# Operand rows of two attentions fetched from SBUF head by head instead of through DRAM

## The reference

```python
def _L0_attn_a_ref(x, Wq, Wk, Wv, Wo):        # windowed attention
    q, k, v = (proj(Wq), proj(Wk), proj(Wv))
    scores = jnp.einsum('bnsd,bntd->bnst', q, k) * scale
    mask = _longformer_mask(S)                # |i - j| <= 16, token 0 sees all and is seen by all
    scores = jnp.where(mask[None, None], scores, jnp.float32(-jnp.inf))
    attn = jax.nn.softmax(scores, axis=-1)
    out = jnp.einsum('bnst,bntd->bnsd', attn, v)
    return jnp.einsum('bsh,oh->bso', out.transpose(0, 2, 1, 3).reshape(B, S, H), Wo)
...
    x = x + windowed attention; + ternary FFN; + bidirectional gated recurrence; + ternary FFN
    x = x + full attention (_L1_attn_a_ref); x = x + mixture of experts
    x = x + full attention (_L1_attn_b_ref); x = x + mixture of experts
```

## Time and profile before

| | |
|---|---|
| median of 3 runs | 1111.35 us |
| profiled execution | 1111.73 us, its span 1110.0 us, mean granted TensorE clock 0.94 |
| TensorE (PE) busy | 1001.4 us, 90% |
| VectorE (DVE) busy | 833.8 us, 75% |
| ScalarE (ACT) busy | 747.5 us, 67% |
| GpSimd (POOL) busy | 154.9 us, 14% |
| DMA | 60386 packets, 64.47 MB, mean 58 GB/s; HBM read 27.06 MB, written 35.32 MB |

### The profile page before, as it was taken

How to read it: one execution, slowest core, us unless ns; L and a number is a source line. 1 busy time by engine, 2 the same in 40 slices (tenths; PEclk the granted TensorE clock), 3 DMA queues, 4 the chain that set the end, 5 groups by cost and what they waited for, 6 DMA issues and landing times.

```text
span 1110.0 us, 32515 instructions
## 1 busy us (share of the span) xinstructions
PE 1001.4 (90%) x13424; PEld 460.4 (41%) x13437; DVE 833.8 (75%) x1030; ACT 747.5 (67%) x1490; POOL 154.9 (14%) x430
## 2 busy tenths in 40 slices
PE   6699999688769999999899899999989999999897
PEld 2445455333342344444344344434434344443344
DVE  4546654447647999999778789977879997898732
ACT  3514446265440999998767789876779986697781
POOL 8200000036000000000102110010211001010000
PEclk8889999889869999999989899989999998999899
DMA  3753442100044323201000044200004420010000
GB/s 105 211 180 86 109 103 60 37 0 1 1 146 141 70 51 77 56 18 27 14 10 15 20 129 105 57 12 13 13 23 129 106 53 12 12 40 21 11 26 24
DMA packets 60386, 64.47 MB, mean 58 GB/s; under 512 B 17424, under 2 KB 39184, under 8 KB 60112
## 3 DMA queue, kind: packets, MB, share of 16 engines
q1 hardware_dynamic: 60240, 62.40, 21.3%
HBM read 27.06 MB, written 35.32 MB: 56 GB/s over the span
## 4 chain that ended last, share of the span: by engine, by line
DVE 51%; PE 37%; ACT 4%; DMA 3%; issue 3%; SPq 1%; ACTq 0%; DVEq 0%
DVE nmf L1670 42%; PE wide L685 24%; PE bank L685 13%; DVE xcsq L1441 1%; DMA KQs<-mw_dram 1%; ACT L1196 1%; DVE xp L1441 1%; ACT big L1196 1%; ACT scr L1196 1%; DVE xcsq L1450 1%; SPq L445 1%; DVE nmt L1609 1%; DMA x<-xT 1%; DVE res L1441 1%; DVE big L1822 0%
## 5 line engine op out<-in xcount | busy, mean ns | idle before, releaser
L1670 DVE TENSOR_REDUCE nmf<-wide 128x1 f32<-128x1024 f32 x512 | 591.2, 1209 | 54.7 <-PE wide L685 54.2
L1196 ACT ACTIVATE big<-wide 128x512 f32<-128x512 f32 x683 | 391.4, 601 | 100.7 <-PE wide L685 90.0
L685 PE MATMUL wide<-big,KQs 48*128 48x512 bf16 (+1 forms) x1376 | 359.7, 351 | 4.3 <-DVE nmf L1670 3.0
L685 PE MATMUL bank<-big,V 128*9 128x128 f32 x8192 | 329.5, 280 | 11.2
L685 PE MATMUL wide<-KQs,big 50*128 50x512 bf16 (+1 forms) x1035 | 274.2, 331 | 8.1 <-ACT big L1196 8.1
L685 PEld LDWEIGHTS bank<-big,V 128*9 128x9 f32 x8192 | 178.2, 91 | 239.0 <-ACT big L1196 188.8
L1196 ACT ACTIVATE big<-bank 128x512 f32<-128x512 f32 (+1 forms) x469 | 232.7, 515 | 46.8 <-PE bank L685 41.3
L685 PE MATMUL bank<-KQs,big 50*128 50x512 bf16 x341 | 133.8, 392 | 3.9 <-ACT big L1196 3.9
L685 PEld LDWEIGHTS wide<-KQs,big 50*128 50x128 bf16 x1035 | 70.1, 95 | 116.5 <-ACT big L1196 61.7
L1196 ACT ACTIVATE scr<-wide 128x380 f32<-128x380 f32 (+3 forms) x128 | 61.2, 486 | 81.2 <-PE wide L685 70.0
L618 POOL CAST nms<-nmf 128x4 bf16<-128x4 f32 x128 | 23.8, 186 | 651.8 <-DVE nmf L1670 651.8
(11 more groups left out here) (214 smaller groups left out, 802.7 us busy)
## 6 DMA issues: line engine op xcount, KB each, us to landing
o_dram<-big SPq DMA_DIRECT2D x128, 64.0 KB
big<-kf_dram SPq DMA_DIRECT2D x32, 200.0 KB
kf_dram<-scr SPq DMA_DIRECT2D x24, 256.0 KB, 3.4
qf_dram<-scr SPq DMA_DIRECT2D x24, 256.0 KB, 3.7
KQs<-qf_dram SPq DMA_DIRECT2D x32, 192.0 KB
ow_dram<-scr SPq DMA_DIRECT2D x32, 142.5 KB
big<-kw_dram SPq DMA_DIRECT2D x16, 275.0 KB
kw_dram<-scr SPq DMA_DIRECT2D x12, 352.0 KB, 5.6
```

The costliest lines, as they stand in the source:

```text
L685: return nc.tensor.matmul(o, l, r, start=start, stop=stop, **kw)
L1196: return nc.scalar.activation(o, i, f, **kw)
L1670: nc.vector.tensor_reduce(nmf[:, i % 4, c:c + 1], wide[:, k:k + 2, :].rearrange("p g c -> p (g c)"), AX.X, ALU.max, negate=True).then_inc( ...
```

## The change

The four DRAM tensors of operands and all stores into them go. A part tensor now has four blocks instead of three: the first part stands twice (`AGAIN`), in such an order (`BLOCK`) that the six products of q's and k's parts are two runs of three adjacent blocks on each side. One DMA (`rows_in`) reads three adjacent blocks of one head's 8 partitions and writes 24 operand rows; a head takes two DMAs for k and two for q. The rows of ones are written into the operands directly. Batch 1's parts get buffers of their own (in `big` and `xcsq`; `s0` and `xwin` move). SP's order is rewritten: windowed, the heads of batch 0 at once when its parts are there, those of batch 1 one a unit; full, twelve heads of batch 0 before the first shift, then one a slot, and batch 1's in slots 4 to 15; in layer 2 one head a slot from slot 19 of the run on.

Beside this: the repeated first part is copied by VectorE (windowed, in `third`) and by POOL (full, `fp_again`, `c_again`); token 0's scores are six bf16 products of parts instead of one fp32 product with `kf`; ScalarE waits for all 16 heads of batch 0 (`op_in`) before its first windowed weight; fillers go from 22 to 8 and from 24 to none; `true_x` runs before `project_full`, and TensorE's first full maxima no longer wait for batch 1's residues.

```diff
-ROW_PARTS = ((2, 1, 0, 1, 0, 0), (0, 1, 2, 0, 1, 0))
+BLOCK = ((1, 2, 3), (2, 1, 0))
+AGAIN = (0, 3)
+PRODUCTS = ((3, 2), (2, 2), (2, 1), (1, 2), (1, 1), (1, 0))
...
-        partk = partw[:, 0:3 * KW].rearrange("p (n c) -> p n c", n=3)
-        partq = partw[:, 3 * KW:3 * (KW + QW)].rearrange("p (n c) -> p n c", n=3)
+        partk = [blocks(scr, 0, KW), blocks(big, o, KW)]
+        partq = [blocks(scr, 2 * KW, QW), blocks(xcsq, 0, QW)]
...
-        partf = scr[:, 0:3072].bitcast(BF16).rearrange("p (n i c) -> p n i c", n=2, i=3)
+        partf = [[blocks(t, 2 * S * i, S) for i in range(2)] for t in (scr, xcsq)]
...
+        HEADS = [4 * g + odd + 2 * j for g in range(H // 4) for odd in range(2) for j in range(2)]
...
+            def ones_rows_in(t):
+                cols = t.shape[1] * t.shape[2] // 64
+                for r in (KR, KR + 1, 64 + KR, 64 + KR + 1):
+                    row = t[r:r + 1, :, :].rearrange("r n c -> r (n c)").rearrange("r (a c) -> r a c", c=cols)
+                    sp.dma_start(row, onesb[:, 0:cols]).then_inc(ones_in, 16)
+
+            def rows_in(dst, r, k, h, src, signal):
+                for a in range(2):
+                    o = a if k else 1 - a
+                    sp.dma_start(dst[r + KR // 2 * a:r + KR // 2 * (a + 1)], src[D * h:D * h + D, o:o + 3, :]).then_inc(signal, 16)
...
+                def load_head(b, h):
+                    p, r, s = h // 2, 64 * (h % 2), op_in[2 * (4 * b + h // 4) + h % 2]
+                    rows_in(kopw[:, p, KW * b:KW * b + KW], r, 0, h, partk[b], s)
+                    rows_in(qopw[:, p, QW * b:QW * b + QW], r, 1, h, partq[b], s)
...
+                sp.wait_ge(part3, 2 * len(WG))
+                for h in HEADS[0:H // 2]:
+                    load_head(0, h)
                 sp.wait_ge(win_const, 1)
                 for u in range(AHEAD_W - 1):
+                    for h in HEADS[H // 2 + 2 * u:H // 2 + 2 * u + 2]:
+                        load_head(0, h)
                     turned(u, mw_dram[u, :, :])
                     if u:
                         shift(u - 1)
...
-                    if u in LOADS_W:
-                        load_group(LOADS_W[u])
+                    if u < H + 3 and u % 6 != 5:
+                        load_head(1, HEADS[u - (u + 1) // 6])
...
+                sp.wait_ge(fp_first, 1)
+                ones_rows_in(kop)
+                sp.wait_ge(fp_third, 4)
+                sp.wait_ge(fp_again, 4)
+                for h in HEADS[0:H - 4]:
+                    load_full(0, h, partf[0])
                 pair(0)
                 for i in range(ALL_SLOTS):
                     if i % 2 == 0 and i + 2 < ALL_SLOTS:
                         pair(i + 2)
-                    if i in LOADS:
-                        load_group(LOADS[i])
+                    if i < 4:
+                        load_full(0, HEADS[H - 4 + i], partf[0])
+                    if i == 4:
+                        sp.wait_ge(fp_third, 8)
+                        sp.wait_ge(fp_again, 8)
+                    if 4 <= i < 16:
+                        for h in HEADS[4 * (i - 4) // 3:4 * (i - 3) // 3]:
+                            load_full(1, h, partf[1])
...
-                            for j in range(3):
-                                store_parts(r, (o - STORE) // 2, (o - STORE) % 2 * 3 + j)
-                        if o in LOAD:
-                            load_batch(r, LOAD.index(o))
+                        o = i - START[r] // 4 - LOAD
+                        if 0 <= o < H:
+                            load_batch(r, o)
...
+                    pool.tensor_copy(o[:, AGAIN[k], :], o[:, BLOCK[k][0], :]).then_inc(c_again, 1)
...
-                    ins = mm(bk(3 + t // 5)[0:H, 0:k * QT].rearrange("p (t k) -> p t k", k=QT),
-                             q0m[:, b, :], cols[:, :, HALF:HALF + QT])
+                    for n, (i, j) in enumerate(PRODUCTS):
+                        cols = partk[b][:, i, t * P:(t + k) * P].rearrange("p (t k) -> p t k", k=P)
+                        ins = mm(o, q0m[:, b, j, :], cols[:, :, HALF:HALF + QT], start=(n == 0), stop=(n == 5))
...
-                keep_busy(2, bk(6))
-                keep_busy(20, bk(7))
+                keep_busy(8, bk(7))
...
-                keep_busy(24, bk(7))
                 for i in range(AHEAD):
...
+                pe.wait_ge(fp_res, 8)
+                pe.wait_ge(fp_v, NC)
+                pe.wait_ge(ones_in, 128)
                 for tick in range(END):
...
             def windowed_attention():
-                for k in range(2):
-                    act.wait_ge(partw_out[k], 96 * B)
+                for j in range(2 * GROUPS):
+                    act.wait_ge(op_in[j], 128)
...
-                        if b and at == 0:
-                            act.wait_ge(partw_out[int(kind == "q")], 96)
...
-                        if c == 2:
-                            act.wait_ge(part_out[k], 96 * (2 * layer - 1))
...
+                def third(m, r, o, k):
+                    nc.vector.tensor_copy(o[:, AGAIN[k], :], o[:, BLOCK[k][0], :])
                     dve.wait_ge(part2, m + 1)
...
                 if stage == 4:
+                    true_x()
                     project_full(1)
-                    true_x()
                     full_attentions()
```

More of the change, by code:

```diff
@@ L190, in build @@
         part2, part3, part_v = sem("part2"), sem("part3"), sem("part_v")
-        partw_out = [sem(f"partw_out{i}") for i in range(2)]
+        q0_parts = sem("q0_parts")
         q0_max = sem("q0_max")
@@ L199, in build @@
         fp_second, fp_third, fp_v = sem("fp_second"), sem("fp_third"), sem("fp_v")
-        part_out = [sem(f"part_out{i}") for i in range(2)]
-        ones_rows, ones_out = sem("ones_rows"), sem("ones_out")
+        fp_again, c_again = sem("fp_again"), sem("c_again")
+        ones_rows, ones_in = sem("ones_rows"), sem("ones_in")
         sc_ready, sc_exp = sem("sc_ready"), sem("sc_exp")
@@ L436, in windowed_attention @@
                         if u == H + 3:
+                            for j in range(2 * GROUPS, 4 * GROUPS):
+                                sp.wait_ge(op_in[j], 128)
                             batch_in(0)
@@ L440, in windowed_attention, with load_full @@
                 batch_in(1)
-            def store_full(k, b, j):
-                dst = (qf_dram if k else kf_dram)[j * D:j * D + D, :, S * b:S * b + S].rearrange("d h c -> h d c")
-                sp.dma_start(dst, partf[:, k, ROW_PARTS[k][j], :]).then_inc(part_out[k], 16)
-            def load_full(b, k, odd, p0, p1, group):
-                dst, src, rows = (qop, qf_dram, KR) if k else (kop, kf_dram, KR + 2)
-                r = 64 * odd
-                sp.dma_start(dst[r:r + rows, p0:p1, S * b:S * b + S],
-                             src[:, 2 * p0 + odd:2 * p1:2, S * b:S * b + S]).then_inc(op_in[group], 16)
-            def full_attentions():
-                def load_group(g):
-                    b, p0 = g // GROUPS, g % GROUPS * 2
-                    for odd in range(2):
-                        for k in range(2):
-                            load_full(b, k, odd, p0, p0 + 2, 2 * g + odd)
+            def load_full(b, h, parts):
+                p, r, s = h // 2, 64 * (h % 2), op_in[2 * (GROUPS * b + h // 4) + h % 2]
+                for k, t in enumerate((kop, qop)):
+                    rows_in(t[:, p, S * b:S * b + S], r, k, h, parts[k], s)
+            def full_attentions():
                 def shift(i):
@@ L650, in _ @@
                     recurrent()
+            for i, c, m in halves(1):
+                if i != "v":
+                    q, at = int(i == "q"), 512 * (c % 2)
+                    o = partf[c // 2][q][:, :, at:at + 512]
+                    pool.wait_ge(fp_first, m + 1)
+                    pool.tensor_copy(o[:, AGAIN[q], :], o[:, BLOCK[q][0], :]).then_inc(fp_again, 1)
             def chain(r, name):
@@ L1235, in project_window @@
                 for b in range(B):
-                    act.copy(xwin[:, b, :, P - 1:P],
+                    act.copy(xwin[b][:, :, P - 1:P],
                              xp[:, b, HALF:HALF + 1].unsqueeze(1).broadcast_to((P, WT, 1))).then_inc(win_first, 1)
@@ L1265, in project_window @@
                     if kind != "v":
-                        before = m, res[:, m % CBUF, 0:cols], o[:, 1, :]
+                        before = m, res[:, m % CBUF, 0:cols], o[:, BLOCK[k][1], :]
                         m += 1
@@ L1523, in project_window @@
                     if kind != "v":
-                        o, r = (partk if kind == "k" else partq)[:, :, at:at + cols], res[:, m % CBUF, 0:cols]
+                        q = int(kind == "q")
+                        o, r = (partk, partq)[q][b][:, :, at:at + cols], res[:, m % CBUF, 0:cols]
                         dve.wait_ge(part1, m + 1)
@@ L1532, in project_window @@
                     if kind != "v":
-                        before = m, r, o
+                        before = m, r, o, q
                         m += 1
```

(9 more changed lines are left out.)

166 lines of the change are left out of this document (56 added, 110 removed).

## The result

The changed kernel takes **1228.97 us** (median of 4 runs, 1226.19 to 1231.34) where the kernel before took 1112.57 beside it: ratio **1.1047**, 95% interval 1.1015 to 1.1080. The direction was forecast, the size was not: +116 us for +21, and 51 us past the upper end of the range.

A forecast was written before the change was run, and what follows sets the result against it. It saw VectorE's full-attention row maximum holding 42% of the chain, TensorE most of the rest. Fetch delays of 16.1 (windowed), 2.1 (layer 1's start) and 3 (its slots) gave +21.2 us: 1133 us, range 1088 to 1178.

The forecast's parts named there:

- Removed waits: ScalarE's four waits for batch 0's part stores in the two projections vanish: 8.3 us windowed, 8.2 us full.
- Issue, 0.56 us: SP's cost to issue one fetch between SBUF partitions, gap included; 2.24 us a head.
- Transfer, 61 GB/s: Fetch rate, reckoned by the 24 rows written; a head takes 3.83 us windowed, 3.20 us full.
- rival (c): The narrow source, 8 partitions on two ports, binds: 4.3 us a head windowed, 3.6 full; 1156 us; chance 0.17.
- Batch 0's windowed operands: ScalarE's first windowed weight waits for all 16 fetched heads: 101.7 us where it stood at 85.63, +16.1 us.
- The loop of 19 units: Windowed, batch 1's 16 heads take 61.3 us within 61.6: no loss, up to 8 us if the lead's cover went.
- five units of lead: Windowed loop: 16 us of lead was to cover the 8 us by which SP's own time exceeds 19 units.
- Layer 1's start: Full stage: first shift, behind twelve heads' fetches, sets first scores at 361.2 instead of 359.07 us: +2.1 us.
- Slots 4 to 15: Full stage, layer 1: fetches take 4.27 of 4.57 us a slot and delay shifts: +3 us, between 0 and 15.
- Layer 2, hidden, 0: Full stage, layer 2: one head's fetch a slot, 3.20 of 4.57 us, costs nothing.
- (a): Rival: fetches are bound by their issue as queued transfers overlap; -17.7 us, 1094 us; chance 0.30.

The follow-up runs named there:

- run 1: Kernel before plus batch 1's own buffers, true_x first and bf16 zero scores; operands still through DRAM, fillers 22 and 24: 1116.73 us, ratio 1.0049.
- run 2: Kernel with own buffers and operands through DRAM, fillers lengthened from 22 to 38 and 24 to 60: 1100.82 us, ratio 0.9895 to the kernel before.
- run 5: Changed kernel with eight series of DMAs added behind its last store, on an idle chip: 0.666 us an issue, 1.34 us reading always the same 8 partitions.
- run 4: Changed kernel with each windowed fetch moving only 32 of its 1408 or 1045 columns, same number of DMAs and rows: 1192.71 us (one run).
- run 6: Changed kernel with the same fetches reordered, four heads in turns, so successive DMAs read different groups of 8 partitions: 1166.61 us, ratio 1.0477.
- run 10: Changed kernel with 50 filler products put ahead of the full maxima: 1228.74 us, ratio 1.1033.
- run 9: Changed kernel, four heads' fetches in turns, windowed shifts on GpSimd's queue, full-stage fetches between a pair's shift store and loads on SP: 1133.87 us, ratio 1.0202.
- run 7: Changed kernel with shift stores and loads of both attentions issued by GpSimd on its own queue instead of SP: 1476.72 us, ratio 1.3309.

## Why the prediction was wrong, step by step

- **Removed waits** (8.3 + 8.2 us): right, they are gone, and from the last windowed maximum to slot 0 it is 152.2 us for 160.6. That none of it is worth more than the operands allow was right as well; run 1 shows the form it takes, a wait and the clock behind it. With filler up to the operands, run 2 is 13 us faster than before, so the waits were worth something by themselves.
- **Issue, 0.56 us**: wrong, 0.67 + 0.04 alone (run 5). The nearest row was L393's 0.62 us, and 0.52 was taken from a form that never had SBUF on both sides.
- **Transfer, 61 GB/s**: the number was near while batch 0 was fetched (58 GB/s from 38 to 104 us), the reason was not right. (The 56 GB/s of the loop count the output stores too.) It was reckoned by the rows written; it is the 8 partitions read, in four fetches running, which is rival (c)'s mechanism. The reason matters: by rows written no order of the fetches would help, by the partitions read the order gives 62 us back.
- **Batch 0's windowed operands**: first weight forecast at 101.7, stood at 105.8, +20.2 us for +16.1. By the forecast's own sum that is (105.8 - 2.0 - 37.7)/16 = 4.13 us a head, between its 3.83 and rival (c)'s 4.3.
- **The loop of 19 units, "it just fits", 0 to 8 us**: this is the step that failed, with about +39 us (59.1 - 20.2). SP's own time was set at 3.66 us a unit. It is 4.8 to 5.0 in a unit with a head where the issues go at their own price (runs 4 and 6: 2.9 for the head, 0.56 + 0.64 + 0.57 for the others, and gaps), and mostly 6 to 8 where the transfers hold up the issues. At the issues' own price, as an estimate, 16 heads at 2.88 and 19 times 0.56 + 0.64 + 0.57 + 0.12 are 82 us for the 61.6 of the 19 units, 20 over. Run 6 shows all of it: from first weight to last maximum it takes 115.9 us for 95.7. The five units of lead (16 us), which were to cover 8, covered none. The rest of the +39 came with the slow transfers. The sum took transfer and issue as two bounds side by side, 3.83 and 2.24 a head; in one queue the slow transfers also lengthen the issues of the stores. And the 61.3 us for 16 heads counted no bytes but theirs, where each unit's output store moves 142.5 KB through the same queue.
- **Layer 1's start**: the first scores stood at 422.5, 63.4 us later than before and 4.3 more than the windowed stage had brought (forecast +2.1). The forecast had them wait for the first shift and hid the slow clock behind it. It was the other way round: with the clock restored (run 10) they stood at 418.5 and waited for the shift, so some 0.3 of the 4.3 us are the shift's way and 4.0 the clock's. In the whole time run 10 does not show these 4.0.
- **Slots 4 to 15, +3 us, at most 15**: the same error; +30.6 up to slot 24. The bound of 15 had the right picture, fetches and the shift's way in series, 11.5 us for 9.14. It left out the output stores and the slower issues.
- **Layer 2, hidden, 0**: wrong, +10.7 and +9.3 us. One head a slot was compared with the slot, 3.20 for 4.57 us, but SP has to get a whole pair done in 9.14: two heads, two outputs, a store, its landing and two loads are 11.8. Some 4 us of each figure may be scatter (run 9, where the granted clock over these slots was 0.90 and 0.93 for 0.93 and 0.98 in run 6).
- **Rivals**: (a), bound by issue alone, forecast 1094; with issue alone, or nearly so, as the bound (run 6) it is 1167. With the issue as measured its sum up to the first weight holds: 38.4 + 64 x 0.71 + 4.1 + 2 = 89.9, for 89.65 in run 6. Its error is the price and, for the most part, the same loop. (c), 1156, had the right mechanism and the start to 4 us, and missed the loop too.

## What to carry to other kernels

Where one queue issues everything, add up for one turn of the loop all that it does in order (each issue, each wait for a landing) and compare that sum with the turn; a transfer that is "hidden" per item can still break the loop. Let DMAs that follow each other read from different partition groups: here the order alone was worth 5% of the time. And where a wait ahead of TensorE is taken away, look at its clock: here it then stood 7.6 us, the four slots behind ran at 1.2 GHz, and filler up to the operands' arrival brought 16 us (1116.7 to 1100.8).

## What was not expected of the hardware

- The fetches between SBUF partitions cost SP 0.666 us to issue with 1.5 or 67.6 KB alike (run 5). With 24 rows on each side it is 0.714, with 8 it is 0.625 (median of 48); group loads from DRAM cost 0.33 to 0.36.
- 16 such DMAs from one group of 8 partitions: 50 GB/s; from 16 groups: 78, with the issue as the bound. The DMA share was 0.44 and 0.40 there, 0.77 with 16 partitions and 0.91 with 128 (series 3, 1, 4 and 6).
- The granted clock stayed at 0.50 for some 31 us of first maxima although TensorE shows as busy in nearly all of them (run 1); in the kernel before it was 0.50 from 324 to 330 us and 0.88 on average from 336 to 342, behind the filler's start.
- DMAs on GpSimd's queue landed in 2.3 and 1.8 us (medians) in the full stage and a store of the same size in 4.5 us in the windowed one (run 7).
